# One gated cross-attention and feed-forward block: a new order of VectorE's first statistics, and two normalisations a step later

## The chip, the cores and the metric

The kernel runs on one core of one Trainium2 chip. A time is the device time of one execution in microseconds (us). Of the kernel before there are three timed runs and one profiled execution. TensorE is PE in the profile (PEld are its weight loads), VectorE is DVE, ScalarE is ACT, GpSimd is POOL, SyncE is SP.

## The reference, cut to what matters

There are four sequences (b = 0 to 3) of 256 tokens and 256 features.

```python
def _layernorm(x, eps=1e-5): return (x - mean(x)) / sqrt(var(x) + eps)

# attention over the context; x only supplies the values
query, key = ctx @ Wq.T + bq, ctx @ Wk.T + bk
attention = softmax(einsum('bnd,bmd->bnm', query, key), axis=-1)
x = x + tanh(g_xattn[0]) * einsum('bln,bmn->blm', _layernorm(x), attention)

# feed-forward on the new x, matmuls on e4m3 operands with bf16 results
h = _layernorm(x)
gate, up = qdot(h, w_gating[0]), qdot(h, w_gating[1])      # 256 -> 1024
x = x + tanh(g_ffn[0]) * qdot(gelu(gate) * up, w_linear)    # 1024 -> 256
```

## The kernel before, in words

**First half, per sequence b.** TensorE projects the context into a query and a key (`project_q`, `project_k`); ScalarE copies the query out of PSUM with its bias (`q_out`), VectorE the key (`k_out`, line 422). Two row tiles of energies follow on TensorE (`energy`, line 577: four matmul instructions of 128x256 in float32). VectorE takes the negated row maximum of both tiles in one instruction (`row_max`, line 427), ScalarE the exponentials with their sums (`exps`, line 326), VectorE one over the sum (`invert_sum`, line 432), GpSimd multiplies (`normalise`, line 273), TensorE transposes (line 593) and multiplies with x (`attend`, line 606). In between, VectorE takes the statistics of x: `stats1` (line 413) per row tile and `moments1` (line 418) per sequence; GpSimd turns those of a pair of sequences into factors (`scales1`). The order on VectorE is written out by hand, call by call; every instruction waits in that order, and what stands behind a waiting one waits too. `s_x[b]`, `k_done`, `energy_done` and `exp_ready` are the semaphores that `stats1`, `k_out`, `row_max` and `invert_sum` wait for.

The key projection of sequence 2 goes into the bank of sequence 0 (`k_b[b % 2]`), and `energy(2)` waits for `k_out(2)`. TensorE's order is projections 0 and 1, `energy(0)`, `energy(1)`, projections 2 and 3, `energy(2)`, the transposes of sequence 0, `energy(3)`, and so on.

**Second half.** `add_attention` on VectorE gives x2; `stats2` and `moments2` its mean and variance; GpSimd computes the reciprocal root (`rstd2`, line 264) and, for sequences 0, 2 and 3, the shift (line 268). The normalised rows xh are made on ScalarE for sequences 0, 2 and 3 (`norm2`, line 345, two instructions) and on VectorE for sequence 1. TensorE transposes xh (`turn_x2`, line 627, four small matmuls) and ScalarE copies the result out as xq (`xq_out`, line 351). The feed-forward part is a list of 20 steps: steps 0 and 1 do hidden tile 0 for sequences 0 and 1 apart, steps 2 to 8 hidden tiles 1 to 7 for both together, step 9 is the first of sequences 2 and 3, steps 9 to 13 do their tiles 0 to 4, and steps 14 to 19 are halves of the last three tiles. Step s is, on TensorE, `ffn1(s)`: two gate matmuls (line 645) and two up matmuls (line 651), then `ffn2(s - 3)` (line 671, four matmuls of a full step). ScalarE does `gelu(s)` (line 360), VectorE `product(s)` (line 467) and `round_product(s - 1)` (line 476). `ffn1(s)` waits for `gelu(s - 2)` before its gate matmuls and for `product(s - 2)` before its up matmuls; `gelu(s)` waits for `product(s - 2)`. Step 9 waits for xq of sequences 2 and 3.

**X_AFTER** is a pair of steps: after `ffn1` and `ffn2` of step X_AFTER[0] TensorE does `turn_x2(2)`, after those of X_AFTER[1] `turn_x2(3)`. On ScalarE `norm2(2)` stands behind `gelu(X_AFTER[0] - 1)` and `xq_out(2)` behind `gelu(X_AFTER[0])`; the same with X_AFTER[1] for sequence 3. Three `shift_x2` (line 339) stand behind the gelus of the three steps after X_AFTER[1]. VectorE's `moments2(2)` stands in step 1 and `moments2(3)` in step 3.

Of the kernel before, what the change touches and what calls it, by code (L numbers as in the profile page):

```python
# [33 lines left out]
def flamingo_block(nc, params_ctxT, x, xT, w_gating, w_linear, out):  # L34

    B, _, LT, D = x.shape
    KC, L = xT.shape[2], xT.shape[3]
    C = params_ctxT.shape[0]  # L40
    NPAR = 2 * C + 4
    WK = P + L
    BIAS = WK + P
    NWG, _, _, _, WCOLS = w_gating.shape
    HT = w_linear.shape[1]
    assert L == LT * P and D == KC * P and C == P and 2 * L == 512
# [17 lines left out]
    STEPS += [divmod(n, HT) + (0, GB) for n in range(FIRST, G * HT - SPLIT)]  # L64
    STEPS += [(G - 1, j, i, i + 1) for i in range(GB) for j in range(HT - SPLIT, HT)]
    S = len(STEPS)
    X_AFTER = (4, 6)
    ACT_NORM = (0, 2, 3)

    ctx = ExitStack()  # L70
    with ctx:  # L71
# [59 lines left out]
        def halves(t):  # L131
            return t[:, :].rearrange("p (a c) -> p a c", a=2)
# [69 lines left out]
        def last_step(b):  # L202

            return max(s for s, (g, _, i0, i1) in enumerate(STEPS) if GB * g + i0 <= b < GB * g + i1)
# [106 lines left out]
        def _(act):  # L311
# [22 lines left out]
            def shift_x2(n):  # L334
                b, t = ((2, 0), (3, 0), (3, 1))[n]
                if n == 0:
                    act.wait_ge(nms1_ready, 1)
                act.wait_ge(x2_ready, LT * b + t + 1)
                nc.scalar.activation(x2s[:, n], x2[:, b, t], ACT.Identity,
                                     bias=nms1[:, b, t:t + 1]).then_inc(x2s_ready, 1)  # L340

            def norm2(b):
                act.wait_ge(nmr2_ready, ACT_NORM.index(b) + 1)
                for t in range(LT):
                    nc.scalar.activation(xh[:, b, t], x2[:, b, t], ACT.Identity, bias=nmr2[:, b, t:t + 1],  # L345
                                         scale=r2[:, b, t:t + 1], saturate=False).then_inc(act_xh_ready, 1)

            def xq_out(b):
                act.wait_ge(xh_turned, b + 1)
                g, o = b // GB, (b % GB) * L  # L350
                nc.scalar.activation(xq[:, g, :, o:o + L], halves(x2_b[b]), ACT.Copy,
                                     saturate=False).then_inc(xq_ready, 1)

            def gelu(s):
                _, _, i0, i1 = STEPS[s]
                toks = slice(i0 * L, i1 * L)
                act.wait_ge(gate_done, s + 1)
                if s >= 2:
                    act.wait_ge(prod_ready, s - 1)
                nc.scalar.activation(gl[:, s % 2, toks], gate_b[s % 2][:, toks],  # L360
                                     ACT.Gelu_apprx_tanh).then_inc(gelu_ready, 1)
# [26 lines left out]
            for s in range(S):  # L388
                gelu(s)
                if s == X_AFTER[0] - 1:  # L390
                    norm2(2)
                if s == X_AFTER[1] - 1:
                    norm2(3)
                if s == X_AFTER[0]:
                    xq_out(2)
                if s == X_AFTER[1]:
                    xq_out(3)
                if X_AFTER[1] < s <= X_AFTER[1] + LT + 1:
                    shift_x2(s - X_AFTER[1] - 1)
                if s == first_of_g1 + LAG:  # L400
# [8 lines left out]
        def _(dve):  # L409
            def stats1(b, t):  # L410
                if t == 0:
                    dve.wait_ge(s_x[b], 16)
                nc.vector.bn_stats(st1[:, b, t], x_sb[:, b, t]).then_inc(st1_ready, 1)

            def moments1(b):
                for t in range(LT):
                    dve.wait_ge(st1_ready, LT * b + t + 1)
                    nc.vector.bn_aggr(mv1[:, b, t], st1[:, b, t]).then_inc(mv1_ready, 1)

            def k_out(b):  # L420
                dve.wait_ge(k_done, b + 1)
                nc.vector.tensor_scalar(kT[:, b * L:(b + 1) * L], k_b[b % 2][:, 0:L], bk, None,  # L422
                                        ALU.add).then_inc(k_ready, 1)

            def row_max(b):
                dve.wait_ge(energy_done, b + 1)
                nc.vector.tensor_reduce(nmax[:, b], halves(enrg[b]), AX_X, ALU.max,  # L427
                                        negate=True).then_inc(max_ready, 1)

            def invert_sum(b):  # L430
                dve.wait_ge(exp_ready, LT * (b + 1))
                nc.vector.reciprocal(rsum[:, b], esum[:, b]).then_inc(rsum_ready, 1)  # L432
# [57 lines left out]
            nc.vector.tensor_scalar(ntg[:, :], tg[:, 0:1], -1.0, None, ALU.mult).then_inc(ntg_ready, 1)  # L490
            nc.vector.tensor_scalar(yscale[:, :], tg[:, 1:2], 1.0 / ACT_SCALE, None, ALU.mult).then_inc(yscale_ready, 1)
            k_out(0)
            stats1(0, 0)
            stats1(0, 1)
            moments1(0)
            k_out(1)
            row_max(0)
            row_max(1)
            invert_sum(0)
            k_out(2)  # L500
            stats1(1, 0)
# [245 lines left out]
```

## Time and profile before

| | us |
|---|---|
| median of three runs | 49.26 (49.19, 49.26, 49.66) |
| the profiled execution | 49.57 |
| its span, first to last instruction | 47.8 |
| PE busy | 42.6 (89%), 246 matmuls |
| DVE busy | 34.2 (72%) |
| ACT busy | 29.3 (61%) |
| POOL busy | 18.7 (39%) |

The profiled execution was 0.31 us longer than the median. Busy time of PE is modelled for pipelined matmuls: each matmul's own duration overlaps the next one's, so TensorE's pace is read from start to start. Instructions of VectorE and ScalarE overlap their successors a little too. Mean granted clock of TensorE over the span was 0.981 of full.

### The profile page before, as it was taken

How to read it: one execution, taken by the hardware profiler on the slowest of the kernel's cores; microseconds unless marked ns; L12 is line 12 of the kernel's file. 1: busy time of each engine (PE TensorE's matmuls, PEld its weight loads, DVE VectorE, ACT ScalarE, POOL GpSimd, SP SyncE). 2: the span in 40 equal slices, each digit the busy share in tenths (PEclk: the TensorE clock that was granted, in tenths of full speed). 3: DMA queues.
4: the chain of work that ended last, by engine and by line, in shares of the span. 5: the costliest groups of instructions: out<-in, count | busy, mean ns of one | idle time of the engine just before them, and what ended most of it. 6: DMA issues, size and time to landing. Idle time of an engine off the chain costs nothing.

```text
span 47.8 us, 853 instructions
## 1 busy us (share of the span) xinstructions
PE 42.6 (89%) x246; PEld 28.9 (60%) x246; DVE 34.2 (72%) x107; ACT 29.3 (61%) x66; POOL 18.7 (39%) x41
## 2 busy tenths in 40 slices
PE   3999998999999999999996999999999999999000
PEld 1318758878888898774452555656565687863000
DVE  0101495899899997988899975776666999599700
ACT  0641433993990699677649999778447994564000
POOL 3200899168989896800070700000000895002300
PEclk9999999999999999999999999999999999999975
DMA  0499899999999950000000000000000033600092
GB/s 0 71 361 354 292 377 389 346 189 122 93 104 105 106 55 3 0 0 14 7 0 0 0 0 0 0 7 0 0 0 0 0 117 109 226 0 0 0 340 99
DMA packets 3605, 4.64 MB, mean 97 GB/s; under 512 B 401, under 2 KB 2321, under 8 KB 3601
## 3 DMA queue, kind: packets, MB, share of 16 engines
q1 hardware_dynamic: 2448, 3.61, 22.3%
q0 software_dynamic: 864, 0.79, 17.9%
q10 hardware_dynamic: 288, 0.20, 1.4%
q8 instruction: 2, 0.03, 0.3%
q14 instruction: 3, 0.02, 0.1%
HBM read 5.90 MB, written 1.05 MB: 145 GB/s over the span
## 4 chain that ended last, share of the span: by engine, by line
PE 67%; DVE 10%; DMA 6%; issue 5%; ACT 2%; POOL 2%; DVEq 2%
PE bank L606 15%; PE bank L671 13%; PE bank L645 10%; PE bank L651 10%; PE bank L577 6%; DMA par<-params_ctxT 6%; PE bank L561 4%; PE bank L593 4%; PE bank L569 3%; DVE ap L467 3%; PE bank L627 2%; DVE kT L422 2%; POOL r L264 2%; DVEq L71 2%; DVE x L438 1%
## 5 line engine op out<-in xcount | busy, mean ns | idle before, releaser
L467 DVE SCALAR_TENSOR_TENSOR ap<-bank,gl 128x512 f16<-128x512 f32 (+1 forms) x20 | 11.6, 581 | 4.2 <-PE bank L651 3.4
L360 ACT ACTIVATE gl<-bank 128x512 bf16<-128x512 f32 (+1 forms) x20 | 10.2, 510 | 4.7 <-PE bank L645 4.4
L651 PE MATMUL bank<-xq,wg 128*128 128x512 fp8e4 (+1 forms) x40 | 10.2, 337 | 0.0
L645 PE MATMUL bank<-xq,wg 128*128 128x512 fp8e4 (+1 forms) x40 | 10.2, 336 | 0.0
L671 PE MATMUL bank<-wl,aq 128*128 128x256 fp8e4 x64 | 9.9, 273 | 0.2
L671 PEld LDWEIGHTS bank<-wl,aq 128*128 128x128 f16 x64 | 6.0, 98 | 3.9 <-DVE aq L476 0.9
L606 PE MATMUL bank<-attnT,xT_sb 128*128 128x256 f32 x32 | 7.8, 383 | 0.0
L279 POOL TENSOR_TENSOR yo<-ys,x 128x256 f32<-128x256 f32 x4 | 2.9, 749 | 9.8 <-ACT ys L368 9.8
L476 DVE TENSOR_SCALAR aq<-ap 128x512 uint16<-128x512 uint16 (+1 forms) x20 | 6.1, 310 | 0.0
L606 PEld LDWEIGHTS bank<-attnT,xT_sb 128*128 128x128 f32 x32 | 5.7, 190 | 0.6
L651 PEld LDWEIGHTS bank<-xq,wg 128*128 128x128 fp8e4 x40 | 3.7, 98 | 3.5 <-DVE ap L467 1.2
L264 POOL TENSOR_TENSOR r<-ve,neg_half 128x2 f32<-128x2 f32 x4 | 2.9, 717 | 5.6 <-DVE ve L450 5.6
L326 ACT ACTIVATE e<-bank,nmax 128x256 f32<-128x256 f32 x8 | 3.7, 479 | 1.6 <-DVE nmax L427 1.6
L577 PE MATMUL bank<-kT,qT 128*128 128x256 f32 x16 | 4.3, 390 | 0.1
L273 POOL TENSOR_SCALAR attn<-e,rsum 128x256 f32<-128x256 f32 x8 | 3.7, 478 | 1.7 <-DVE rsum L432 1.5
L645 PEld LDWEIGHTS bank<-xq,wg 128*128 128x128 fp8e4 x40 | 3.7, 98 | 0.8
L242 POOL DMA_DIRECT2D wg<-w_gating x4 | 2.5, 623 | 3.5 <-DMA par<-params_ctxT 3.5
L438 DVE SCALAR_TENSOR_TENSOR x<-bank,s,x_sb 128x256 f32<-128x256 f32 x8 | 3.5, 476 | 0.5 <-PE bank L606 0.4
L345 ACT ACTIVATE xh<-x,nmr,r 128x256 fp8e4<-128x256 f32 x6 | 3.3, 592 | 0.8 <-POOL nmr L268 0.7
L332 ACT COPY attnT<-bank 128x512 f32<-128x512 f32 x4 | 2.3, 583 | 2.3 <-PE bank L593 2.3
L555 PE MATMUL bank<-const-bfloat16-1.0 128*128 128x512 bf16 x6 | 2.7, 626 | 0.8 <-PEq L739 0.8
L577 PEld LDWEIGHTS bank<-kT,qT 128*128 128x128 f32 x16 | 2.7, 189 | 1.1 <-issue 0.9
(47 smaller groups left out, 55.0 us busy)
## 6 DMA issues: line engine op xcount, KB each, us to landing
x_sb<-x SPq DMA_DIRECT2D x4, 256.0 KB, 4.5
xT_sb<-xT SPq DMA_DIRECT2D x4, 256.0 KB, 5.6
out<-yo SPq DMA_DIRECT2D x6, 128.0 KB, 2.0
wg<-w_gating POOLq DMA_DIRECT2D x4, 128.0 KB, 9.0
par<-params_ctxT SPq DMA_DIRECT2D x1, 256.0 KB, 4.2
wl<-w_linear POOLq DMA_DIRECT2D x2, 128.0 KB, 9.0
out<-yo SPq DMA_DIRECT2D x1, 256.0 KB, 2.0
par<-params_ctxT SPq DMA_DIRECT2D x1, 192.0 KB, 2.8
```

What stands on the lines that cost most here:

```text
L264: nc.gpsimd.tensor_tensor(r2[:, b], ve2[:, b], neg_half[:, 0], ALU.pow).then_inc(r2_ready, 1)
L273: nc.gpsimd.tensor_scalar(attn[:, b, t], e[:, b, t], rsum[:, b, t:t + 1], 1.0, ALU.mult, ALU.mult).then_inc(pool_attn_ready, 1)
L326: nc.scalar.activation(e[:, b, t], halves(enrg[b])[:, t], ACT.Exp, bias=nmax[:, b, t:t + 1], accum_out=esum[:, b, t:t + 1]).then_inc(exp_r ...
L360: nc.scalar.activation(gl[:, s % 2, toks], gate_b[s % 2][:, toks], ACT.Gelu_apprx_tanh).then_inc(gelu_ready, 1)
L438: nc.vector.scalar_tensor_tensor(x2[:, b, t], halves(pv_b[b % 2])[:, t], s1[:, b, t:t + 1], x_sb[:, b, t], ALU.mult, ALU.add).then_inc(x2_ ...
L467: nc.vector.scalar_tensor_tensor(ap[:, s % NAP, toks], up_b[s % 2][:, toks], ACT_SCALE, gl[:, s % 2, toks], ALU.mult, ALU.mult).then_inc(p ...
L476: nc.vector.tensor_scalar(aq[:, s % NAQ, toks].bitcast(U16), ap[:, s % NAP, toks].bitcast(U16), ROUND_TO_E4M3, ROUND_TO_E4M3, ALU.add, ALU ...
L577: mm = nc.tensor.matmul(halves(enrg[b])[:, t], qT[:, m:m + P], kT[:, b * L:(b + 1) * L], start=True, stop=True)
L606: mm = nc.tensor.matmul(halves(pv_b[b % 2])[:, t], xT_sb[:, b, k, t * P:(t + 1) * P], attnT[:, b, k], start=(k == 0), stop=(k == KC - 1))
L645: mm = nc.tensor.matmul(gate_b[s % 2][:, toks], wg8[:, c, k, 0, o:o + P], xq[:, g, k, toks], start=(k == 0), stop=(k == KC - 1))
L651: mm = nc.tensor.matmul(up_b[s % 2][:, toks], wg8[:, c, k, 1, o:o + P], xq[:, g, k, toks], start=(k == 0), stop=(k == KC - 1))
L671: mm = nc.tensor.matmul(halves(y_b[g][i])[:, t], aq[:, s % NAQ, m:m + P], wl8[:, j], start=(j == 0 and t == 0), stop=(j == HT - 1), skip_g ...
```

## The change

```diff
-    X_AFTER = (4, 6)
+    X_AFTER = (5, 7)
...
             k_out(0)
+            k_out(1)
+            row_max(0)
             stats1(0, 0)
             stats1(0, 1)
+            row_max(1)
             moments1(0)
-            k_out(1)
-            row_max(0)
-            row_max(1)
             invert_sum(0)
             k_out(2)
```

The number of instructions is the same on every engine; SP's and GpSimd's orders are the same as before.

On VectorE, near the start (kT is the key, st1 and mv1 the statistics of x, nmax the row maximum; bank7 and bank5 hold keys 0 and 1, bank2 and bank3 energies 0 and 1):

```order
 L422 TENSOR_SCALAR kT<-bank7,par 128x256
-L413 BN_STATS st1<-x_sb 128x6 x2
-L418 BN_AGGR mv1<-st1 128x2 x2
 L422 TENSOR_SCALAR kT<-bank5,par 128x256
 L427 TENSOR_REDUCE nmax<-bank2 128x2
+L413 BN_STATS st1<-x_sb 128x6 x2
 L427 TENSOR_REDUCE nmax<-bank3 128x2
+L418 BN_AGGR mv1<-st1 128x2 x2
 L432 RECIPROCAL rsum<-esum 128x2
 L422 TENSOR_SCALAR kT<-bank7,par 128x256
```

The second key and the first maximum now precede sequence 0's statistics, and the aggregation follows the second maximum; between `k_out(0)`, the first row, and `k_out(2)`, the last, stand the same eight instructions as before.

On TensorE, in the feed-forward steps (L627 are the transposes, first of sequence 2 into bank6, then of sequence 3 into bank7):

```order
-L627 MATMUL bank6<-ident8,xh 128x128 x4
 L645 MATMUL bank3<-xq,wg8 128x512 x2
 L651 MATMUL bank5<-xq,wg8 128x512 x2
 L671 MATMUL bank0<-wl8,aq 128x256 x2
 L671 MATMUL bank1<-wl8,aq 128x256 x2
+L627 MATMUL bank6<-ident8,xh 128x128 x4
 L645 MATMUL bank2<-xq,wg8 128x512 x2
 L651 MATMUL bank4<-xq,wg8 128x512 x2
 L671 MATMUL bank0<-wl8,aq 128x256 x2
 L671 MATMUL bank1<-wl8,aq 128x256 x2
-L627 MATMUL bank7<-ident8,xh 128x128 x4
```

Sequence 2's transposes moved behind the matmuls of step 5 (the first five rows); sequence 3's move in the same way behind those of step 7.

On ScalarE at the same place (gl is the gelu's output, xh the normalised rows; the rows from `gelu(3)` on):

```order
 L360 ACTIVATE gl<-bank3 128x512
+L360 ACTIVATE gl<-bank2 128x512
 L345 ACTIVATE xh<-x2,nmr2,r2 128x256 x2
+L360 ACTIVATE gl<-bank3 128x512
+L351 ACTIVATE xq<-bank6 128x2x256
 L360 ACTIVATE gl<-bank2 128x512
-L351 ACTIVATE xq<-bank6 128x2x256
+L345 ACTIVATE xh<-x2,nmr2,r2 128x256 x2
 L360 ACTIVATE gl<-bank3 128x512
```

`gelu(4)` now stands ahead of sequence 2's normalisation, and `gelu(5)` ahead of its copy `xq_out(2)`; sequence 3 and the three shifts follow one step later too.

## Rows read from the trace of the kernel before

**Rows 1.** Table by stretches: busy us (and instructions) of PE, PEld, DVE, ACT, POOL, then granted clock, DMA share, GB/s
```profile
10.00:21.00 11.00, 11.00 (x65) 9.44 (x65) 10.37 (x39) 7.99 (x21) 8.53 (x18) 1.00 0.75 76
25.16:26.17 1.01, 0.56 (x7) 0.26 (x6) 1.01 (x5) 1.01 (x3) 0.00 (x0) 1.00 0.00 0
26.17:31.59 5.42, 5.42 (x38) 3.36 (x37) 3.86 (x11) 5.00 (x11) 0.91 (x2) 1.00 0.00 0
```

**Rows 2.** Timeline of PE and PEld, start: start us, length us, engine, line, operation, count [idle]
```profile
5.68 0.59 PE L569 MATMUL bank<-par 128*128 128x256 f32 x2
6.12 2.31 PE L577 MATMUL bank<-kT,qT 128*128 128x256 f32 x8
...
7.30 0.73 PEld L577 LDWEIGHTS bank<-kT,qT 128*128 128x128 f32 x4 [0.51 <-issue]
...
9.99 1.07 PE L577 MATMUL bank<-kT,qT 128*128 128x256 f32 x4
```

**Rows 3.** Timeline of DVE, the first keys, statistics and maxima
```profile
5.86 0.74 DVE L413 BATCH_NORM_STATS2 st<-x_sb 128x6 f32<-128x256 f32 x2
6.51 0.30 DVE L418 BATCH_NORM_AGGREGATE mv<-st 128x2 f32<-128x6 f32 x2
6.73 0.45 DVE L422 TENSOR_SCALAR kT<-bank,par 128x256 f32<-128x256 f32 x1
7.23 0.69 DVE L427 TENSOR_REDUCE nmax<-bank 128x2 f32<-128x512 f32 x1
8.47 0.69 DVE L427 TENSOR_REDUCE nmax<-bank 128x2 f32<-128x512 f32 x1 [0.55 <-PE bank L577]
9.08 0.15 DVE L432 RECIPROCAL rsum<-esum 128x2 f32<-128x2 f32 x1
9.33 0.48 DVE L422 TENSOR_SCALAR kT<-bank,par 128x256 f32<-128x256 f32 x1
...
10.60 0.15 DVE L432 RECIPROCAL rsum<-esum 128x2 f32<-128x2 f32 x1
10.67 0.41 DVE L413 BATCH_NORM_STATS2 st<-x_sb 128x6 f32<-128x256 f32 x1
```

**Rows 4.** Timeline of ACT and of POOL, second sequence's exponentials and normalisation
```profile
9.27 0.47 ACT L326 ACTIVATE e<-bank,nmax 128x256 f32<-128x256 f32 x1
...
10.85 0.93 POOL L273 TENSOR_SCALAR attn<-e,rsum 128x256 f32<-128x256 f32 x2 [0.48 <-DVE rsum L432]
```

**Rows 5.** Timeline of PE, feed-forward steps 4 to 7
```profile
24.08 0.59 PE L645 MATMUL bank<-xq,wg 128*128 128x512 fp8e4 x2
...
24.94 0.38 PE L671 MATMUL bank<-wl,aq 128*128 128x256 fp8e4 x2
25.64 0.69 PE L627 MATMUL bank<-ident,xh 128*128 128x128 fp8e4 x4 [0.32 <-ACT xh L345]
26.17 0.59 PE L645 MATMUL bank<-xq,wg 128*128 128x512 fp8e4 x2
...
28.77 0.39 PE L627 MATMUL bank<-ident,xh 128*128 128x128 fp8e4 x4
28.99 0.59 PE L645 MATMUL bank<-xq,wg 128*128 128x512 fp8e4 x2
```

**Rows 6.** Timeline of ACT, POOL and DVE beside these steps
```profile
24.90 1.09 ACT L345 ACTIVATE xh<-x,nmr,r 128x256 fp8e4<-128x256 f32 x2 [0.67 <-POOL nmr L268]
25.90 0.57 ACT L360 ACTIVATE gl<-bank 128x512 bf16<-128x512 f32 x1
...
26.34 0.16 DVE L452 TENSOR_SCALAR nm<-mv 128x2 f32<-128x2 f32 x1
26.56 0.69 DVE L467 SCALAR_TENSOR_TENSOR ap<-bank,gl 128x512 f16<-128x512 f32 x1
...
27.29 0.21 POOL L268 TENSOR_TENSOR nmr<-nm,r 128x2 f32<-128x2 f32 x1
...
29.19 0.60 ACT L351 ACTIVATE xq<-bank 128x512 fp8e4<-128x512 f32 x1
```

## The prediction

> **What bounds the kernel now.** I read the table by stretches first. From 10.00 to 21.00 TensorE is busy for 11.00 of 11.00 us, and again for 5.42 of 5.42 us from 26.17 to 31.59; between 25.16 and 26.17 it has 0.56 us of work in 1.01 us, at a granted clock of 1.00 in all three [rows 1]. The reader is to see that TensorE sets the pace, and that one hole lies in the middle of the feed-forward part. The timeline of the first stage shows a second, smaller hole: the weights of the second energy are loaded at 7.30 after 0.51 us of idle weight loading [rows 2], 0.12 us after the second key was done at 6.73 + 0.45 = 7.18 [rows 3]. The change touches both holes. What matters is whether a hole closes, or only moves to the next wait.
>
> **The later transposes (X_AFTER), the main term.** TensorE's two matmuls of `ffn2(1)` start at 24.94. A row of two 128x256 matmuls is half the columns of one of two 128x512 (0.43 us from start to start, below), so they occupy 0.22 us, and TensorE is free at 25.16. The transposes of sequence 2 begin only at 25.64, wait once more in their middle for ScalarE's second normalised half (0.32 us idle is put to ACT), and the gate matmuls of step 5 start at 26.17 [rows 5]. Four unhindered transposes take 28.99 - 28.77 = 0.22 us [rows 5]. So the hole is 26.17 - 25.16 - 0.22 = 0.79 us. Its cause is the normalisation on ScalarE, which started at 24.90 after 0.67 us of waiting for GpSimd, and took until 25.99 [rows 6].
>
> In the new order step 5 comes first. Its gate matmuls need `gelu(3)`, which was over before ScalarE's wait that ended at 24.90 began, so they start at 25.16. Two pairs of 128x512 at 0.43 each (24.08 to 24.94 is two pairs [rows 5]) and four matmuls of 128x256 in `ffn2(2)`, 0.43, bring TensorE to 26.46 at the transposes. ScalarE meanwhile: `gelu(4)` can start when its gate matmuls are done, 24.08 + 0.59 = 24.67 [rows 5], plus some 0.04; it takes 0.57, with the next starting 0.1 before its end (25.90 to 26.37 is 0.47 in the old order). The normalisation thus starts near 25.2 instead of 24.90 and its second half is ready 1.09 later, at 26.3 [rows 6]. That is 0.15 us ahead of the transposes at 26.46, so their stall goes entirely.
>
> What is late next is the product of step 4 on VectorE, for which `ffn1(6)`'s up matmuls wait. It ran at 26.56 after `gelu(4)`; `gelu(4)` is now done by 25.3, but VectorE itself is still in `moments2(3)`, whose last row starts at 26.34 [rows 6] and leaves it free at about 26.41. The product then ends at 26.41 + 0.69 = 27.10. TensorE asks for it at 26.46 + 0.22 + 0.43 = 27.11, and a semaphore took 0.12 above: 0.05 us of the gain is lost. After this, at steps 6 to 9: ScalarE does `gelu(5)` at 26.2, `xq_out(2)` at 26.9, `gelu(6)` at 27.4, the second normalisation from 27.9 to 28.95, `gelu(7)` to 29.4; TensorE comes to sequence 3's transposes at 27.16 + 0.43 + 0.43 + 0.86 + 0.43 = 29.3, after their rows are ready. `xq_out(3)` starts 0.42 behind the transposes (29.19 against 28.77) and takes 0.60 [rows 5, 6], until 30.35. Step 9 needs it at 29.3 + 0.22 + 1.30 = 30.85. It is hidden with 0.5 us to spare; without that cover each late tenth would be lost. The three shifts and everything behind them only fill ScalarE's idle time. Term: 0.79 - 0.05 = **-0.74 us**, bounded by -0.79 (product in time) and by -0.4 (ScalarE half a normalisation behind).
>
> **The new order on VectorE at the start.** The second key can be copied when its projection ends, 5.68 + 0.59 = 6.27 [rows 2]: from 6.3 to 6.8 instead of 6.73 to 7.18. The second energy then follows the first without the hole, TensorE gets to projections 2 and 3 some 0.35 us earlier, and has them done by 9.65 instead of 9.99. But `energy(2)` waits for `k_out(2)`, that is for VectorE. From start to start: the first maximum stays at 7.23, since it waits for the first energy, which began at 6.12 in both (the second, 7.30 to 8.47, shows the same 1.15 from weights to maximum); the maximum takes 8.47 to 9.08 = 0.61; two statistics 6.51 - 5.86 = 0.65; the second maximum 0.61; two aggregations 6.73 - 6.51 = 0.22; the reciprocal 0.07 (10.60 to 10.67) [rows 3]. 7.23 + 0.61 + 0.65 + 0.61 + 0.22 + 0.07 = 9.39 for `k_out(2)` against 9.33 [rows 3]. VectorE's idle time of 0.55 ahead of the second maximum is filled with statistics, but new idle time ahead of the second key and the first maximum takes its place. So `energy(2)` starts 0.06 us later than 9.99 [rows 2], and as TensorE has no idle time from there to 21 [rows 1], the whole chain moves by this. The second maximum ends at 8.49 + 0.69 = 9.18, before ScalarE gets to the second exponentials at 9.27 [rows 4], so they don't move; GpSimd's second normalisation (10.85 [rows 4]) stays within 0.1 of its place. Term: **+0.06 us**, bounded below by 0 (a kernel in which `k_out(2)` is bound by its projection gains nothing here, since what TensorE wins it waits away) and above by the case in which VectorE's instructions don't overlap.
>
> That upper bound has a rule to it. In this trace the first statistics end at 5.86 + 0.74 = 6.60 while the next row starts at 6.51, and the maximum of 8.47 ends at 9.16 with the reciprocal at 9.08 [rows 3]: successors start 0.08 early. With full durations (0.69, 0.74, 0.69, 0.30, 0.15) `k_out(2)` would start at 7.23 + 2.57 = 9.80, a term of +0.47 instead of +0.06. The Trainium skill, page "VectorE: DVE Perf Modes", section "The DRAIN you can't avoid", says that the next operation does not start until the pipe of the one before is empty. By that rule, the trace disagrees in every row pair just named, so I take the start-to-start figures and keep the rule's outcome as a rival.
>
> **Sum.** -0.74 + 0.06 = -0.68 us. The profiled execution of 49.57 would become 48.89; against the median of the runs shown, 0.31 lower, it is 49.26 - 0.68 = **48.58 us**, 1.4% less. What this kernel's measurement can tell from no change is about 1%, 0.49 us, so anything from 48.77 to 49.75 counts as the same.
>
> **The rivals.**
> 1. *VectorE doesn't overlap in the new order*, as by the rule above: -0.74 + 0.47 gives 49.0, the same within 1%. Against it stand the row pairs; for it, that a maximum read from PSUM directly ahead of statistics read from SBUF is none of them. Chance 0.06.
> 2. *The hole moves instead of closing*: ScalarE has 5.00 us of work in the 5.42 us from 26.17 to 31.59 [rows 1], now with a gelu ahead of each normalisation. If it is 0.3 to 0.4 us later than I work out, the transposes or the product stall again for half of the 0.79: 49.26 + 0.06 - 0.4 = 48.9, the same within 1%. For it: only 0.15 us of slack at sequence 2's transposes. Against it: the rows give each start. Chance 0.17.
> 3. *The start gains*: if `k_out(2)` is not late and the first maximum can be had before 7.23, the energies move up by 0.1 to 0.3 us, 48.3. Against it: the first maximum began 0.05 us after the key ahead of it ended, where unhindered successors start 0.08 early, so it did wait for its energy. Chance 0.08.
> 4. *Both transposes stall*, slower than before: sequence 3's normalisation needs GpSimd's shift, ready at 27.29 + 0.21 = 27.50 [rows 6], and I have ScalarE at it at 27.9. If VectorE's statistics of sequence 3 came over 0.4 + 0.4 us later (slack at the shift, slack at the transposes), the second pair of transposes would stall as the first does now, while the first keeps its stall: 49.26 + 0.06 + 0.79 = 50.1. It decides only when the shift is ready after 28.3; nothing in the new order delays VectorE's statistics by that. Chance 0.04.
>
> **How the numbers follow.** The forecast has 0.65. The range of its own case is 48.4 to 48.85. Rivals 1 and 2 lie at 48.9 to 49.0, rival 3 at 48.3; the range from 48.2 to 49.2 takes them in with the bounds of the terms and leaves out rival 4 and the scatter of single runs. Faster by over 1% (below 48.77): nine tenths of the forecast and rival 3, 0.59 + 0.08 = 0.67, less a little for scatter, 0.64. Within 1%: the rest of the forecast and rivals 1 and 2, 0.31. Slower: 0.05.
>
> **What would show it.** In the changed kernel: no idle time between `ffn2(1)` and the gate matmuls of step 5; the four transposes of each sequence close together, like the 0.39 row; a gap of at most 0.1 us ahead of the up matmuls of step 6; step 9 without a wait for xq. At the start: the second energy directly behind the first, then about 0.35 us of idle time ahead of `energy(2)` where there was none, and `k_out(2)` at 9.4. The forecast is wrong if the transposes of sequence 2 still carry an idle time put to ACT, if `energy(2)` starts more than 0.2 us from its old place, or if the stretch from 31.59 on, which I leave as it is, changes its length.

## The result and the profile after

Over 20 runs of each on the same chips the changed kernel took 48.83 us (median, 48.28 to 49.40) and the kernel before 49.39 (48.84 to 49.90). The ratio is 0.989, with a 95% interval from 0.985 to 0.993: 0.55 us faster, between 0.34 and 0.75. Ratios and their intervals here and below compare only those runs of each kernel that lie within 1.5% of its fastest. The forecast was 0.68 us and 48.58 us, with a range of 48.2 to 49.2. The changed kernel's profiled execution took 49.35 us, its span is 47.6 us.

Table by stretches of the changed kernel, the columns as in [rows 1]; the stretches run from the third energy to the first gate matmuls, and from the gate matmuls of step 5 to those of step 9:

```profile
10.47:21.60 11.13, 11.13 (x65) 9.50 (x66) 10.47 (x39) 8.16 (x21) 8.78 (x19) 1.00 0.69 65
25.67:31.37 5.70, 5.70 (x43) 3.44 (x40) 4.64 (x15) 5.25 (x12) 1.01 (x2) 1.00 0.00 0
```

The second stretch, which answers to the hole and the one after it in [rows 1], took 5.70 us where 25.16 to 31.59 was 6.43 before. TensorE is busy in all of it. Its timeline in the changed kernel, against [rows 5]:

```profile
25.45 0.38 PE L671 MATMUL bank<-wl,aq 128*128 128x256 fp8e4 x2
25.67 0.59 PE L645 MATMUL bank<-xq,wg 128*128 128x512 fp8e4 x2
...
26.97 0.39 PE L627 MATMUL bank<-ident,xh 128*128 128x128 fp8e4 x4
27.19 0.59 PE L645 MATMUL bank<-xq,wg 128*128 128x512 fp8e4 x2
27.67 0.60 PE L651 MATMUL bank<-xq,wg 128*128 128x512 fp8e4 x2
...
31.37 0.59 PE L645 MATMUL bank<-xq,wg 128*128 128x512 fp8e4 x2
```

The gate matmuls of step 5 start 0.22 us behind `ffn2(1)`, as two matmuls of 128x256 take; the four transposes form one row of 0.39, not 0.69; from gate to up matmuls of step 6 it is 0.48 us instead of 0.43, since the up matmuls' weights wait for a product that ends at 26.93 + 0.68 = 27.61 (the PEld row of 27.66 below). The whole of this part lies 0.51 us later than before (first gate matmuls at 21.60, not 21.09), for a reason that the start shows. Beside them on ScalarE and VectorE, against [rows 6]:

```profile
25.22 0.60 ACT L360 ACTIVATE gl<-bank 128x512 bf16<-128x512 f32 x1 [0.48 <-PE bank L645]
25.71 1.08 ACT L345 ACTIVATE xh<-x,nmr,r 128x256 fp8e4<-128x256 f32 x2
...
30.27 0.60 ACT L351 ACTIVATE xq<-bank 128x512 fp8e4<-128x512 f32 x1 [0.33 <-PE bank L627]
...
26.93 0.68 DVE L467 SCALAR_TENSOR_TENSOR ap<-bank,gl 128x512 f16<-128x512 f32 x1
...
27.66 0.11 PEld L651 LDWEIGHTS bank<-xq,wg 128*128 128x128 fp8e4 x2 [0.37 <-DVE ap L467]
```

ScalarE's normalisation no longer waits for GpSimd: it starts at 25.71, right behind `gelu(4)`, 0.30 us later than before when both are counted from the first gate matmuls, and ends at 26.79, 0.18 ahead of the transposes. The copy of sequence 3 ends at 30.87, 0.50 ahead of step 9.

The start reads differently. TensorE and VectorE of the changed kernel, against [rows 2] and [rows 3]:

```profile
5.30 1.06 PE L561 MATMUL bank<-par 128*128 128x256 f32 x2
6.15 0.75 PE L569 MATMUL bank<-par 128*128 128x256 f32 x2
6.74 1.93 PE L577 MATMUL bank<-kT,qT 128*128 128x256 f32 x8
...
10.47 1.10 PE L577 MATMUL bank<-kT,qT 128*128 128x256 f32 x4
```

```profile
5.54 0.48 DVE L422 TENSOR_SCALAR kT<-bank,par 128x256 f32<-128x256 f32 x1 [1.50 <-PE bank L569]
6.94 0.48 DVE L422 TENSOR_SCALAR kT<-bank,par 128x256 f32<-128x256 f32 x1 [0.91 <-PE bank L569]
7.80 0.69 DVE L427 TENSOR_REDUCE nmax<-bank 128x2 f32<-128x512 f32 x1 [0.38 <-PE bank L577]
8.41 0.74 DVE L413 BATCH_NORM_STATS2 st<-x_sb 128x6 f32<-128x256 f32 x2
9.07 0.67 DVE L427 TENSOR_REDUCE nmax<-bank 128x2 f32<-128x512 f32 x1
...
9.86 0.46 DVE L422 TENSOR_SCALAR kT<-bank,par 128x256 f32<-128x256 f32 x1
```

The first energy starts at 6.74, 0.62 later than in the profile before, although nothing ahead of it was changed: two projection matmuls take 0.85 us from start to start here (5.30 to 6.15), 0.43 us from 5.68 in [rows 2]. So the two spans can't be subtracted as they are. From the first energy on, in pieces:

| us from start to start | before | changed |
|---|---|---|
| start of the span to energy(0) | 6.12 | 6.74 |
| energy(0) to energy(2) | 3.87 | 3.73 |
| energy(2) to the first gate matmuls | 11.10 | 11.13 |
| first gate matmuls to those of step 9 | 10.50 | 9.77 |
| step 9 to the end of the span | 16.2 | 16.2 |

The sum is +0.62 - 0.14 + 0.03 - 0.73 = -0.22, the difference of the spans (47.8 and 47.6, rounded). The feed-forward part gave 0.73 us.

### The profile page after: what moved, and what is told of

The parts are those of the page before. It is cut to its first block, busy times and chain, and to the rows that moved or that the text cites. A ratio compares the mean times of both kernels' runs of the same rounds, so it can differ in the third digit from the quotient of the medians.

```text
span 47.6 us, 853 instructions
## 1 busy us (share of the span) xinstructions
PE 43.0 (90%) x246; PEld 29.4 (62%) x246; DVE 33.8 (71%) x107; ACT 29.1 (61%) x66; POOL 18.8 (40%) x41
## 2 busy tenths in 40 slices
DMA packets 3604, 4.64 MB, mean 98 GB/s; under 512 B 400, under 2 KB 2320, under 8 KB 3600
## 4 chain that ended last, share of the span: by engine, by line
PE 87%; DVE 2%; DVEq 2%; issue 1%; ACT 1%
PE bank L606 15%; PE bank L645 14%; PE bank L651 14%; PE bank L671 14%; PE bank L577 8%; PE bank L561 6%; PE bank L555 6%; PE bank L569 5%; PE bank L593 4%; PE bank L627 2%; DVEq L71 2%; DVE aq L476 1%; DVE ap L467 1%; ACT gl L360 1%; DVE yo L484 0%
## 5 line engine op out<-in xcount | busy, mean ns | idle before, releaser
L422 DVE TENSOR_SCALAR kT<-bank,par 128x256 f32<-128x256 f32 x4 | 1.9, 474 | 2.4 <-PE bank L569 2.4
L561 PE MATMUL bank<-par 128*128 128x256 f32 x8 | 3.5, 527 | 0.0
```

Source lines behind the costliest of these rows:

```text
L561: nc.tensor.matmul(q_b[b % 2][:, 0:L], wqT, cT(b), start=True, stop=True).then_inc(q_done, 1)
```

## The experiments

Where a kernel had several runs its ratio to the kernel before, with a 95% interval, is given; the pieces of the table above come from its profiled execution. For one `X_AFTER` they repeat to 0.01 us in the feed-forward part, whatever the run. The kernel before ran eleven times beside e1 to e4 (median 49.69) and eleven other times beside e5 to e8 (49.57).

### Each edit alone, both together, and VectorE's idle time filled

e1 has the new order on VectorE and `X_AFTER = (4, 6)`; e2 has the old order and `(5, 7)`; e3 is the changed kernel; e4 is this, from the changed kernel:

```diff
             k_out(0)
+            stats1(0, 0)
             k_out(1)
+            stats1(0, 1)
             row_max(0)
-            stats1(0, 0)
-            stats1(0, 1)
-            row_max(1)
             moments1(0)
+            row_max(1)
             invert_sum(0)
```

**e1** expected: 

> VectorE's new order at the start alone, X_AFTER at (4, 6) as before. Theory of the prediction: it is worth nothing or a little less (+0.06 us, and the changed kernel's trace suggests -0.1): ratio to the kernel before 0.997 to 1.002; energy(2) starts 3.7 to 3.9 us after energy(0), 3.87 before; the hole of 0.79 us ahead of step 5 stays. Rival (the head carries a part of the gain): ratio at or under 0.994, and every matmul from energy(2) on earlier by 0.3 us.

**e2** expected: 

> X_AFTER = (5, 7) alone, VectorE's order as before. Theory of the prediction: it carries the whole gain, -0.74 us, ratio 0.985; first gate matmul to step 9's gate matmuls 9.76 us against 10.50 before. Rival (the hole moves): a gain of 0.4 us or less, ratio 0.992 or more, and an idle time ahead of sequence 2's or 3's transposes.

**e3** expected: 

> The changed kernel once more, beside the others on one chip. Theory: its ratio is e2's within 0.003, near 0.985 to 0.989. Rival (the two edits help or hinder each other): its ratio is not the product of e1's and e2's.

**e4** expected: 

> The changed kernel with another order on VectorE: k_out(0), stats1(0,0), k_out(1), stats1(0,1), row_max(0), moments1(0), row_max(1), invert_sum(0), k_out(2). The statistics stand in VectorE's idle times ahead of the second key (0.4 us) and of the first maximum (0.4 us), so that k_out(2) is not held up by them. Theory: energy(2) starts 0.3 us earlier relative to energy(0) than in the changed kernel (3.45 against 3.73 us) and the whole is 0.25 to 0.35 us faster than it, ratio to the kernel before near 0.98. Rival (the exponentials on ScalarE or GpSimd's normalisation set the pace from energy(2) on): energy(2) is earlier, but the feed-forward part starts no earlier.

| | runs | ratio | energy(0) at | energy(0) to (2) | energy(0) to gate | gate to step 9 |
|---|---|---|---|---|---|---|
| before | 11 | 1 | 6.12 | 3.87 | 14.97 | 10.50 |
| e1 | 6 | 1.003 (0.994 to 1.011) | 6.12 | 3.78 | 14.91 | 10.50 |
| e2 | 6 | 0.987 (0.977 to 0.997) | 5.57 | 3.84 | 14.94 | 9.76 |
| e3 | 6 | 0.989 (0.981 to 0.997) | 6.76 | 3.74 | 14.86 | 9.77 |
| e4 | 6 | 0.981 (0.973 to 0.990) | 6.95 | 3.53 | 14.66 | 9.76 |

The later step carries the gain: e2 without the new order is as fast as e3 with it (medians 48.70 and 48.69), and has all of the feed-forward part's gain (10.50 to 9.76). e1 is worth nothing that can be measured. Its profile is the best check of the arithmetic of the start, since its first energy is at 6.12 us as in the profile before. TensorE and VectorE of e1:

```profile
6.12 1.94 PE L577 MATMUL bank<-kT,qT 128*128 128x256 f32 x8
...
9.90 1.10 PE L577 MATMUL bank<-kT,qT 128*128 128x256 f32 x4
```

```profile
6.32 0.48 DVE L422 TENSOR_SCALAR kT<-bank,par 128x256 f32<-128x256 f32 x1 [0.38 <-PE bank L569]
7.23 0.69 DVE L427 TENSOR_REDUCE nmax<-bank 128x2 f32<-128x512 f32 x1 [0.42 <-PE bank L577]
7.84 0.74 DVE L413 BATCH_NORM_STATS2 st<-x_sb 128x6 f32<-128x256 f32 x2
8.50 0.67 DVE L427 TENSOR_REDUCE nmax<-bank 128x2 f32<-128x512 f32 x1
9.09 0.24 DVE L418 BATCH_NORM_AGGREGATE mv<-st 128x2 f32<-128x6 f32 x2
9.24 0.13 DVE L432 RECIPROCAL rsum<-esum 128x2 f32<-128x2 f32 x1
9.29 0.47 DVE L422 TENSOR_SCALAR kT<-bank,par 128x256 f32<-128x256 f32 x1
```

The second key at 6.32, the first maximum at 7.23, the statistics at 7.84 and the second maximum at 8.50 are where the prediction put them. Then the two aggregations took 0.15 us instead of 0.22, the reciprocal 0.05 instead of 0.07, and the second maximum 0.59 instead of 0.61: `k_out(2)` came at 9.29, not 9.39.

e4 puts the same statistics into the waits for the second key and for the first energy. Its `k_out(2)` is held by something else, VectorE of e4:

```profile
8.01 0.69 DVE L427 TENSOR_REDUCE nmax<-bank 128x2 f32<-128x512 f32 x1
8.62 0.24 DVE L418 BATCH_NORM_AGGREGATE mv<-st 128x2 f32<-128x6 f32 x2
8.92 0.69 DVE L427 TENSOR_REDUCE nmax<-bank 128x2 f32<-128x512 f32 x1
9.79 0.17 DVE L432 RECIPROCAL rsum<-esum 128x2 f32<-128x2 f32 x1 [0.18 <-ACT e L326]
9.87 0.47 DVE L422 TENSOR_SCALAR kT<-bank,par 128x256 f32<-128x256 f32 x1
```

It waits 0.18 us for the first exponentials on ScalarE; so energy(0) to energy(2) shrank to 3.53, and not to the expected 3.45. The rest of the kernel followed: 0.20 us less up to the first gate matmuls than e3, where 0.25 to 0.35 was expected.

e8 is e4 again, with other runs of the kernel before beside it.

**e8** expected: 

> The kernel with VectorE's filled order a second time. Theory: energy(0) to energy(2) 3.53 us and energy(0) to the first gate matmul 14.66 us, whatever the pace at the start; 0.2 us faster than the changed kernel, ratio to the kernel before 0.980 to 0.986. Rival (the first measurement of it was scatter): ratio 0.989 as the changed kernel.

Measured: ratio 0.985 (0.972 to 0.997), median 48.81 against 49.57; energy(0) to energy(2) 3.53, to the first gate matmuls 14.66, as in e4. Both measurements beat the kernel before. That e4's order also beats the changed kernel rests on the profiles' 0.20 us; the runs' intervals overlap. The 14.66 us is also not below what the old order reaches in some executions: e9 and e11, below, have 14.67 and 14.66.

### How much cover the later step has left

e5 is the changed kernel with `X_AFTER = (6, 8)`, e6 with `X_AFTER = (4, 7)`.

**e5** expected: 

> X_AFTER = (6, 8), one step later still. The prediction gave xq_out(3) 0.5 us of cover ahead of step 9 in the changed kernel. With the transposes of sequence 3 directly ahead of step 9 that cover is gone: theory: step 9's gate matmuls wait for 0.42 + 0.60 us of ScalarE's copy plus some 0.1, so first gate matmul to step 9 is 9.77 + 1.0 = 10.7 us and the kernel is 0.9 to 1.1 us slower than the changed one, ratio to the kernel before 1.00 to 1.01. Rival (later is better still, since the product of step 4 no longer holds up step 6): 9.77 us or less.

**e6** expected: 

> X_AFTER = (4, 7) with VectorE's new order: only sequence 3's chain is a step later, sequence 2's stands as before. Theory: the hole belongs to sequence 2's normalisation alone, so 0.79 us of it stay and first gate matmul to step 9 is 10.4 to 10.5 us, as before. Rival (a part of the gain comes from sequence 3's chain, which ScalarE no longer has to do between steps 5 and 7): 10.2 us or less.

TensorE of e5, steps 6 and 9:

```profile
27.20 0.59 PE L645 MATMUL bank<-xq,wg 128*128 128x512 fp8e4 x2
27.90 0.60 PE L651 MATMUL bank<-xq,wg 128*128 128x512 fp8e4 x2
...
31.60 0.39 PE L627 MATMUL bank<-ident,xh 128*128 128x128 fp8e4 x4
32.68 0.60 PE L645 MATMUL bank<-xq,wg 128*128 128x512 fp8e4 x2 [0.69 <-ACT xq L351]
```

Gate to step 9 took 10.85 us, 1.08 more than in the changed kernel; the median was 50.09, the ratio 1.011 (0.997 to 1.025). Step 9 stood 32.68 - 31.60 - 0.22 = 0.86 us for the copy of sequence 3. The other 0.22 us are at step 6: without transposes ahead of it TensorE is there 0.22 us sooner, and waits that much longer for the product of step 4, 27.90 - 27.20 - 0.43 = 0.27 us. So (5, 7) is the best of the three pairs tried that lie two steps apart: with (4, 6) the normalisation is late, with (6, 8) the copy is.

TensorE of e6:

```profile
25.20 0.38 PE L671 MATMUL bank<-wl,aq 128*128 128x256 fp8e4 x2
25.90 0.69 PE L627 MATMUL bank<-ident,xh 128*128 128x128 fp8e4 x4 [0.33 <-ACT xh L345]
...
31.85 0.59 PE L645 MATMUL bank<-xq,wg 128*128 128x512 fp8e4 x2
```

Gate (at 21.34) to step 9 took 10.51 us: the whole hole is back, with sequence 3's chain a step later. Sequence 3's chain a step later is worth nothing by itself; the hole is that of sequence 2's normalisation. The partner, sequence 2's chain alone at (5, 6), was not run. The one execution of e6 took 49.87 us.

### Why the start differs between executions

e7 is the changed kernel with `WARM_UP = 0`, which leaves out the six matmuls of ones; e9 is e7 with VectorE's old order. e10 is e2's kernel, e11 and e12 are the kernel before. e9 to e12 were executed once each, beside one execution of the kernel before at 49.06 us.

**e7** expected: 

> The changed kernel without the six matmuls of ones at the start. In the profiled executions so far the first energy starts between 5.57 and 6.95 us, as the projections ahead of it run at 0.43 or 0.22 us a matmul. Theory: the moment at which TensorE's pace doubles makes the scatter between executions, and without these matmuls it comes later: first energy at 7.5 us or more, 0.5 to 2 us slower than the changed kernel. Rival (the moment has nothing to do with what TensorE did before): no slower, the same scatter.

**e9** expected: 

> e7 with VectorE's old order: no warm-up matmuls, X_AFTER = (5, 7), so that the keys come at TensorE's half pace and VectorE waits for them. Theory: the statistics of the old order then stand in the wait for the second key and cost nothing, while the new order has them between the two maxima: the second maximum starts 0.95 us after the first instead of 1.26, k_out(2) is held only by its projection, and energy(0) to energy(2) takes 4.45 us against 4.62 in e7; the new order loses where the pace doubles late. Rival (the orders are worth the same at any pace): 4.6 us or more.

**e10** expected: 

> The kernel of e2 once more for one look, to have its start at another moment of TensorE's change of pace. Theory: if the pace doubles after 6 us, so that the first energy starts at 6.6 us or later, the second energy follows the first without a hole and energy(0) to energy(2) takes 3.4 to 3.55 us, less than the 3.73 of the changed kernel; if it doubles near 4 or 5 us it is 3.84 to 3.87 as before. Rival: 3.84 or more at either pace.

**e11** expected: 

> The kernel before for one look, for the same reason as e10 and with the same two expectations for energy(0) to energy(2): 3.4 to 3.55 us with a late change of pace, 3.87 with an early one.

**e12** expected: 

> The kernel before for another look; the expectations are those of e11.

e7 had a ratio of 1.014 (1.001 to 1.026) and a median of 50.28 us. TensorE of e7, and then of e9:

```profile
7.24 2.95 PE L577 MATMUL bank<-kT,qT 128*128 128x256 f32 x8
```

```profile
6.21 1.01 PE L569 MATMUL bank<-par 128*128 128x256 f32 x2
7.05 1.94 PE L577 MATMUL bank<-kT,qT 128*128 128x256 f32 x8
```

In e7 the first energy still ran at the slow pace, its four matmuls from 7.24 to 8.94, 0.43 us each; the second took 1.09 us up to the next projection at 10.03, so the pace doubled in it or just ahead of it. energy(0) to energy(2) took 4.62 us, and energy(0) to the first gate matmuls took 15.74 us. By the ratios it was 2.5% slower than e3, about 1.2 us, within what was expected, though its first energy, at 7.24, came sooner than expected. e9 took 49.46 us; in it the pace had doubled by 7.05, so it is no partner for e7, and the comparison of 4.45 with 4.62 us could not be made. But it shows the old order with a late change of pace. The other executions of the old order have other starts:

| old order on VectorE | energy(0) at | second key possible after first | energy(0) to energy(1) | energy(0) to energy(2) | to gate |
|---|---|---|---|---|---|
| before | 6.12 | 0.86 | 1.21 | 3.87 | 14.97 |
| e2 | 5.57 | 0.91 | 1.18 | 3.84 | 14.94 |
| e10 | 6.46 | 1.06 | 1.03 | 3.69 | 14.79 |
| e12 | 5.64 | 1.07 | 1.02 | 3.68 | 14.78 |
| e11 | 5.69 | 1.26 | 0.86 | 3.53 | 14.66 |
| e9 | 7.05 | 1.65 | 0.86 | 3.54 | 14.67 |

The third column is the end of the second key's projection, plus the 0.05 us or less until a waiting key started (6.28 to 6.32 in e1), less the start of the first key. The executions took 48.99 us (e10), 48.83 (e11) and 48.90 (e12).

VectorE of e11, and below it TensorE with one of its weight loads:

```profile
4.64 0.48 DVE L422 TENSOR_SCALAR kT<-bank,par 128x256 f32<-128x256 f32 x1 [0.56 <-PE bank L569]
5.05 0.74 DVE L413 BATCH_NORM_STATS2 st<-x_sb 128x6 f32<-128x256 f32 x2
5.71 0.30 DVE L418 BATCH_NORM_AGGREGATE mv<-st 128x2 f32<-128x6 f32 x2
5.92 0.45 DVE L422 TENSOR_SCALAR kT<-bank,par 128x256 f32<-128x256 f32 x1
```

```profile
3.48 0.70 PE L561 MATMUL bank<-par 128*128 128x256 f32 x2
...
4.72 0.30 PEld L561 LDWEIGHTS bank<-par 128*128 128x128 f32 x2 [0.52 <-DMA par<-params_ctxT]
4.72 0.70 PE L561 MATMUL bank<-par 128*128 128x256 f32 x2
5.26 0.59 PE L569 MATMUL bank<-par 128*128 128x256 f32 x2
5.69 1.93 PE L577 MATMUL bank<-kT,qT 128*128 128x256 f32 x8
...
9.22 1.10 PE L577 MATMUL bank<-kT,qT 128*128 128x256 f32 x4
```

The old order's two statistics and their aggregations keep VectorE from the second key until 5.92 - 4.64 = 1.28 us after the first. The second key can be copied when its projection ends, here at 5.26 + 0.59 + 0.05 = 5.90, 1.26 us after the first key's start. Where that is 0.86 us, as in the profile before, the statistics hold the key up and the hole of [rows 2] opens; where it is 1.26 us or more they hide in a wait, and the second energy follows the first at once (8 matmuls in 1.93 us).

Two different things stretch the time between the keys. In e9 the pace changed late: the second sequence's projections ran slowly (6.21 to 7.05 for a pair). In e11 it changed earlier than in the profile before: the very first pair of projections has 0.70 us, against 1.22 in the profile before. The first key was therefore early, but TensorE then waited for the transfer that brings the second sequence's context: the weights of that projection were loaded at 4.72, after 0.52 us of idle weight loading put to DMA. e12 shows the same, with 0.33 us until 4.67. So the expectation of e11, 3.53 us with a late change of pace and 3.87 with an early one, did not hold: e11 had the small value with an early change, as e9 had it with a late one, and e12, also early, had 3.68, neither of the two.

The new order has no such hole at any pace, but puts the two statistics between the maxima, so that the second starts 1.27 us behind the first (7.80 to 9.07), where it is 0.91 us in e4 (8.01 to 8.92) and in e11 (6.75 to 7.66). Its energy(0) to energy(2) was 3.73 to 3.78 us in five profiles with the energies at full pace (e1, e3, e5, e6 and the changed kernel). So, from energy to energy, it wins up to 0.1 us against the executions like the one I read, and loses 0.2 us against those like e11 and e9. e10 met neither of its two values: with its energy at 6.46 it fell between, at 3.69; the executions sort by the time between the keys, not by when the energy starts.

## Why the prediction was right, by its own steps

**What bounds the kernel** held: TensorE sets the pace, and the larger hole closed.

**The later transposes**, forecast -0.74 us, measured -0.73 (10.50 to 9.77), and the same within 0.01 in all eight profiles with `(5, 7)`. The normalisation was ready 0.18 us ahead of the transposes, forecast 0.15; the product of step 4 cost step 6 0.05 us, as forecast, though the forecast's own figures (the product's end at 27.10, 0.12 for the semaphore, asked for at 27.11) add up to 0.11: the weights were loaded 0.05 us behind the product's end, not 0.12; the cover at step 9 was 0.50 us, forecast 0.5. That the cover is real, e5 shows: taking it away cost 0.86 us. That the hole was sequence 2's, e6 shows. The tail behind step 9 kept its 16.2 us.

**The new order on VectorE**, forecast +0.06 us up to energy(2), measured -0.09 in e1 at the same pace (3.87 to 3.78), -0.06 up to the gate matmuls. The step that was mis-sized is the row of start-to-start times: two aggregations 0.22, the reciprocal 0.07 and the second maximum 0.61. In the old place the aggregations stood right behind the statistics they wait for; behind the second maximum they took 0.15; the reciprocal took 0.05 and the maximum 0.59. That the difference is the wait for the statistics was not tried by itself. These rows make 0.10 of the 0.15 us by which energy(2) came before the forecast's 10.05. The other 0.05 is a binding that the prediction missed: in e1 and in the changed kernel energy(2) starts 0.61 us behind `k_out(2)` (9.29 to 9.90, 9.86 to 10.47), which would be 9.94 for the 9.33 of the kernel before. There TensorE was still in its projections until 9.56 + 0.43 = 9.99, so the key was not what held energy(2), and its 0.06 us can't simply be added to 9.99. TensorE of the kernel before:

```profile
9.56 0.59 PE L569 MATMUL bank<-par 128*128 128x256 f32 x2
```

The mechanism, that TensorE waits away at energy(2) most of what it won at energy(1), held: in e1 the projections are over at 9.19 + 0.43 = 9.62 and energy(2) starts at 9.90, an idle time of 0.28 us where about 0.35 was forecast.

What the step missed altogether is that it priced the order in one execution. The second key's distance from the first, 0.86 us in the profile that I read, is 0.91 to 1.65 in the other executions of the old order, and by the profiles the edit's worth changes its sign with it. By the letter, one of the prediction's own signs of being wrong came up: energy(2) starts at 10.47 in the changed kernel, 0.48 us from its old place. This is the later first energy (0.62) less what was won behind it (0.14), and not the step that the sign was meant for. That the total came within 0.13 us of the forecast is in part luck: +0.06 lies between the -0.09 and the +0.20 that the order is worth in one execution or another, and no step of the prediction had weighed these. The same fits the runs' gain (0.55 us, interval 0.34 to 0.75) being under the 0.84 us that the pieces of the two profiles give from energy(0) on; how often each case comes up was not counted, so that it accounts for the difference is not shown.

**The rivals.** VectorE not overlapping (1) fell: behind the maximum at 7.80 the statistics start at 8.41, and the maximum lasts until 8.49. The Trainium skill, page "VectorE: DVE Perf Modes", section "The DRAIN you can't avoid", has the rule as the prediction told it, that the next operation does not start until the pipe is empty; the same section adds that a next operation that is not held starts earlier, which the prediction left out. These rows agree with the addition: the statistics start 0.08 us before the maximum ends. The hole moving (2) did not happen at (5, 7); e5 shows what it looks like one step further. The start gaining (3) came only to 0.09 us in e1, and its first maximum was not had before 7.23; e4 gets 0.31 us up to the gate matmuls (14.97 to 14.66) by another order, against the execution that was read. Both transposes stalling (4) did not happen: they are rows of 0.39 us.

## What to carry to other kernels

A stall behind a long chain of small operations can be closed, as here, by letting the bounding engine do one more unit of work first; before moving it, work out the cover that is left at the far end, since one step further cost here 1.08 us where the first step had won 0.73. Statistics or other filler work belong into waits that exist at every pace: list the waits of that engine in several executions, and place each piece into one of them. And a price read in one profile holds for that execution's start only; take the pieces between fixed events, not the span, to compare two profiles.

## What the runs showed of the hardware

TensorE's pace at the start differs between executions of one kernel. Two 128x256 float32 projection matmuls take 0.85 us from start to start in the changed kernel's profile (5.30 to 6.15) and 0.43 us once the energies are done (8.51 to 8.94); the eight energy matmuls take 1.77 us (6.74 to 8.51), 0.22 each. The table by stretches gives a granted clock of 1.00 (2.4 GHz) for both stretches below, of which the first holds the slow pair; here the spacing tells more than the column:

```profile
5.30:6.70 1.40, 1.40 (x5) 1.19 (x4) 0.48 (x1) 0.30 (x1) 1.40 (x3) 1.00 1.00 372
6.70:8.50 1.80, 1.80 (x9) 1.45 (x9) 1.18 (x3) 0.17 (x1) 1.63 (x4) 1.00 1.05 401
```

The first stretch has five matmuls in 1.40 us, and the pace changes within it; the second has nine in 1.80. In 13 profiles with energies at full pace the first energy starts anywhere from 5.57 to 7.05 us after the first instruction, and this time goes into the end, since the stretch behind it up to the gate matmuls differs by 0.3 us at most (14.66 to 14.97): of e3's six runs the spans go from 46.5 to 47.6 us. Without the six matmuls of ones ahead (e7) it came later than in any other profile, and the first energy itself ran at the slow pace; e9, also without them, had full pace by its energies, so their absence does not fix the moment. An early change does not always help the start to the full: in e11 TensorE was at the full pace from within the first pair of projections (0.53 us from start to start there, 0.85 in the changed kernel's slow pairs), and then waited for the second sequence's context, so that its first energy (5.69) was no earlier than e2's (5.57).
